# A transformer decoder on one core: copies and tables on ScalarE, reordered TensorE work, and probabilities transposed in two halves of 64 rows

## The chip, the cores and the metric

The kernel runs on one core of a Trainium2 chip. The metric is the device time of one execution in microseconds (us), the median of several runs. Engines are named as in the profile: PE (TensorE; PEld is its weight loading), DVE (VectorE), ACT (ScalarE), POOL (GpSimd), SP (SyncE, which issues the DMAs).

## The reference, cut to what matters

Two batches (B = 2) of 512 tokens with 128 channels pass through six blocks, each added to its input. Two of them have the windowed attention that the change is about: the first (here A) once, and the last (here F) in six layers, each layer followed by a gated feed-forward part on shifted tokens.

```python
def shift_tokens(t):
    a, s = jnp.split(t, 2, -1)
    s = jnp.pad(s, ((0, 0), (1, 0), (0, 0)))[:, :-1]
    return jnp.concatenate([a, s], -1)
...
for i in range(DEPTH):      # DEPTH = 6, HEADS = 16, DIM_HEAD = 64, WINDOW = 32
    x = attn_layer(shift_tokens(x), Wqkv[i], q_scale[i], k_scale[i], Wo[i]) + x
    x = ffn_layer(shift_tokens(x), ln_g[i], ln_b[i], W1[i], b1[i], W2[i], b2[i]) + x
```

`attn_layer` projects to q, k and v, normalises q and k per head, scales them (`q_scale`, `k_scale`), rotates them (with tables of cosine and sine times a position-dependent scale), and lets each token see itself and the 32 before it: scores, softmax, times v, then the output projection. `ffn_layer` is a layer norm, two projections to 341 columns (gate and up), gelu(gate) times up, and a projection back. All is fp32.

## The kernel before, in words

Tokens lie along the free axis: x is [128 channels, 2 x 512]. Block A is two units `("A", b)`, block F twelve units `(("F", l), b)`, one for each layer and batch. Each unit handles 16 heads as 8 pairs p (two heads of 64 channels are 128 partitions). Every engine runs its own program in a fixed order; semaphores join them (`wait_ge` on a mark that another engine's instruction sets). There is no planner: the order in each engine's function is the schedule. `take(pe, bank)` makes PE wait until the readers of a PSUM bank gave it back (`read`).

A unit has three parts. Line numbers are those of the kernel before.

**Projections** (`a_head_*`, `a_proj_*`). For each p PE makes q and k (`a_qk_pe`, L285 and L290, banks p % 2 and 2 + p % 2), now and then a block of v (`a_v_pe`, L274), and in F sums of squares (`a_ss_pe`, L331, bank 5). DVE multiplies q and k with the tables (`a_rope_dve`, L607, L608), SP swaps rows by DMA, POOL adds (L705, L706). Between them runs the feed-forward part of the unit before (`f_before`), placed by hooks: centre (L2015), variance (L2030), three gate/up pairs (`f_up_pe`, L2038 and L2040, banks 6 and 7), on ACT the gelu with table loads around it (L2105, L2109), on DVE `f_mul_dve` (L2159), which frees bank 7, and on PE `f_down_pe` (L2046, three accumulating matmuls to bank 7). Then ACT computes the inverse norms (L513, L515, L516, L518), and PE spreads them to all partitions for pair 0 (`a_spread_q_pe`, `a_spread_k_pe`, L339, rows of 32).

**Steps** (`a_steps_*`), for p = 0 to 7. PE adds the mask to an empty bank (`a_mask_pe`, L372 in 64x64 tiles, L367 for p = 7), adds the scores (`a_scores_pe`, L384, 64x64 tiles), spreads the norms of later pairs (L341, 32 rows, bf16), multiplies the probabilities of p-2 with v (`a_values_pe`, L415, tiles of 128 rows and 64 columns), transposes the probabilities of p-1 (`a_turn_pe`, L398, eight 128x128 transposes), and adds p-3 to the output projection (`a_out_pe`, L425). The mask waits for DVE's subtraction of p-1, the scores for q times its norm. DVE takes the row maximum (`a_top_dve`, L656), subtracts it (L659), multiplies the next pair's q with its norm (L621), sums the exponentials (L642) and inverts (L649). ACT copies k's norm (L534), makes the exponential (L542), copies the values (L547) and the two transposed banks (L554). POOL scales the probabilities (L714) and k (L698). Hooks of the steps: DVE adds the feed-forward result to x after p = 1 (`f_add_dve`, L2164), copies x shifted by one token into `xsh` after p = 3 (`move`, L2133 and L2134), and, for b = 1 and all but the last layer, builds the next layer's four rotation tables after p = 5 (`f_tab_dve`, L2171, four instructions).

**Tail** (`a_tail_*`). Values of p = 6, output of 5, q and k of the next unit's pair 0, transposes of p = 7 and so on, until DVE adds the unit's output to x (L689).

## Time and profile before

| | us |
|---|---|
| median of 3 runs (1751.57 to 1753.41) | 1751.95 |
| the profiled execution | 1752.89 |
| its span in the profile | 1751.1 |
| PE busy | 1573.1 (90%), x15445 |
| DVE busy | 1183.6 (68%), x2048 |
| ACT busy | 904.8 (52%), x1584 |
| POOL busy | 593.2 (34%), x552 |

Block F fills the span from about 830 us to the end, block A the first 150 us. A unit of F repeats almost exactly: measured from one first row maximum (L656, p = 0) to the next unit's, units with b = 0 take 76.3 us and those with b = 1 78.8 us. A matmul's duration in the profile includes its way through the array, so how long PE needs for a piece of work is read from starts: from the start of one group to the start of the next. A plain fp32 matmul appears as two passes ("x2"), a transpose as one.

### The profile page before, as it was taken

Reading aid. Unit: us, or ns where it says so; the run is one execution under the profiler, and the core shown is the slowest. Engines: PE = TensorE matmul, PEld = TensorE weight load, DVE = VectorE, ACT = ScalarE, POOL = GpSimd, SP = SyncE. Lnnn points to the kernel's source line nnn. Section 1 sums busy time; section 2 is a strip of 40 time slices with the busy share of each in tenths; the row PEclk is TensorE's granted clock in tenths of the full one; section 3 lists DMA queues with packets and bytes.
Section 4 is the critical chain, followed back from the end, with each engine's and each line's share of the span. In section 5 each row is a group of like instructions: output and inputs, shape, how many; then the busy total and the mean of one; then the engine's idle time right before and its main releaser. Section 6 shows DMA issues by size and latency. Waiting matters only on the chain.

```text
span 1751.1 us, 37919 instructions
## 1 busy us (share of the span) xinstructions
PE 1573.1 (90%) x15445; PEld 855.6 (49%) x15445; DVE 1183.6 (68%) x2048; ACT 904.8 (52%) x1584; POOL 593.2 (34%) x552
## 2 busy tenths in 40 slices
PE   7887569999999998779999999999999999999996
PEld 2645336565566554223645445363545545353543
DVE  5686576656566654347778778677877867787773
ACT  2435334344533443335665656666566666666663
POOL 5362000000000000105564655445465655555561
PEclk9899779999999999879999999999999999999998
DMA  7134100000000000203041322314142231314120
GB/s 248 28 118 193 54 0 7 2 21 1 21 21 1 21 1 1 93 1 122 30 145 60 96 99 70 129 33 135 56 125 82 86 125 31 127 65 131 68 64 13
DMA packets 50668, 119.41 MB, mean 68 GB/s; under 512 B 15297, under 2 KB 20161, under 8 KB 48321
## 3 DMA queue, kind: packets, MB, share of 16 engines
q1 hardware_dynamic: 50496, 116.99, 20.3%
q8 instruction: 125, 2.05, 0.5%
q14 instruction: 47, 0.38, 0.1%
HBM read 37.52 MB, written 0.52 MB: 22 GB/s over the span
## 4 chain that ended last, share of the span: by engine, by line
PE 52%; DVE 28%; ACT 9%; issue 5%; DMA 3%; POOL 2%; SPq 1%; DVEq 0%; ACTq 0%
DVE nm L656 4%; PE ps L1583 3%; DVE nm L642 3%; PE ps L285 3%; PE ps L425 3%; PE ps L415 3%; PE ps L290 3%; PE ps L1636 3%; PE ps L274 3%; DVE big L659 2%; PE ps L1645 2%; DMA big<-big 2%; DVE big L607 2%; PE ps L1602 2%; DVE big L608 2%
## 5 line engine op out<-in xcount | busy, mean ns | idle before, releaser
L714 POOL TENSOR_TENSOR big<-big,nm 128x384 f32<-128x384 f32 x224 | 189.7, 867 | 186.5 <-DVE nm L649 186.5
L705 POOL TENSOR_TENSOR big<-big 128x512 f32<-128x512 f32 x112 | 143.3, 1280 | 310.8 <-DMA big<-big 309.8
L607 DVE TENSOR_TENSOR big<-ps,big 128x512 f32<-128x512 f32 x224 | 153.7, 686 | 87.3 <-ACT sq L487 55.8
L542 ACT ACTIVATE big<-big 128x384 f32<-128x384 f32 x224 | 109.4, 522 | 126.7 <-DVE big L659 126.6
L1427 POOL MEMSET big<- 128x512 f32 x1 | 0.5, 526 | 489.0 <-DVE x L1910 489.0
L608 DVE TENSOR_TENSOR big<-ps,big 128x512 f32<-128x512 f32 x224 | 152.5, 681 | 0.0
L415 PE MATMUL ps<-big 128*64 128x64 f32 x3584 | 130.6, 226 | 23.1 <-ACT big L554 22.9
L415 PEld LDWEIGHTS ps<-big 128*64 128x64 f32 x3584 | 116.5, 139 | 63.5 <-ACT big L554 46.6
L706 POOL TENSOR_TENSOR big<-big 128x512 f32<-128x512 f32 x112 | 144.5, 1290 | 0.0
L1870 DVE TENSOR_TENSOR big<-ps,fix 128x512 f32<-128x512 f32 x192 | 119.2, 683 | 37.3 <-PE ps L1583 36.9
L398 PE MATMUL ps<-ident,big 128*128 128x128 f32 x896 | 129.3, 283 | 15.2 <-POOL big L714 13.2
L698 POOL TENSOR_TENSOR big<-big 128x512 f32<-128x512 f32 x84 | 107.2, 1276 | 71.7 <-ACT big L534 71.6
L656 DVE TENSOR_REDUCE nm<-ps 128x4 f32<-128x384 f32 x224 | 112.3, 543 | 26.9 <-PE ps L384 24.3
L554 ACT ACTIVATE big<-ps 128x512 f32<-128x512 f32 x224 | 122.3, 594 | 9.8 <-PE ps L398 8.0
L479 ACT ACTIVATE big<-ps 128x512 f32<-128x512 f32 x112 | 66.7, 595 | 112.8 <-PE ps L274 112.8
L398 PEld LDWEIGHTS ps<-ident,big 128*128 128x128 f32 x896 | 97.8, 142 | 40.5 <-POOL big L714 27.3
L659 DVE TENSOR_TENSOR big<-ps,nm 128x384 f32<-128x384 f32 x224 | 113.5, 549 | 0.3
L642 DVE TENSOR_REDUCE nm<-big 128x8 f32<-128x768 f32 x96 | 91.5, 953 | 21.8 <-ACT big L542 20.0
L274 PE MATMUL ps<-big,xsh 128*128 128x512 f32 x192 | 104.7, 628 | 0.0
L384 PE MATMUL ps<-big 64*64 64x96 f32 (+1 forms) x3584 | 97.3, 244 | 5.5 <-DVE big L627 2.2
L285 PE MATMUL ps<-xsh,big 128*128 128x512 f32 x192 | 100.6, 606 | 0.2 <-DVE big L608 0.2
L425 PE MATMUL ps<-fix,big 128*128 128x512 f32 x192 | 99.6, 600 | 0.7 <-ACT fix L547 0.7
(301 smaller groups left out, 2930.9 us busy)
## 6 DMA issues: line engine op xcount, KB each, us to landing
big<-big SPq DMA_DIRECT2D x224, 256.0 KB, 2.4
big<-big SPq DMA_DIRECT2D x112, 128.0 KB, 2.4
big<-in_F_w SPq DMA_DIRECT2D x6, 1536.0 KB, 7.0
big<-in_zero SPq DMA_DIRECT2D x8, 1088.0 KB, 12.5
big<-big SPq DMA_DIRECT2D x84, 64.0 KB, 2.0
big<-in_D_w SPq DMA_DIRECT2D x12, 256.0 KB, 3.0
big<-in_F_wo SPq DMA_DIRECT2D x6, 512.0 KB, 4.3
big<-in_F_w SPq DMA_DIRECT2D x6, 341.0 KB, 3.0
```

The source lines that it names most:

```text
L274: pe.matmul(ps[:, kv, :], src_of(key, b)[:, 128 * t:128 * t + 128], Wqkv[:, 2, 512 * hf:512 * hf + 512], start=True, stop=True).then_inc(* ...
L285: pe.matmul(ps[:, kq, :], Wqkv[:, 0, 128 * p:128 * p + 128], src_of(key, b), start=True, stop=True).then_inc(*full[kq].mark((key, b, "q", p)))
L398: last = pe.transpose(ps[:, 4 + h, 128 * j:128 * j + 128], P[:, 2 * (p % 2) + h, at0:at0 + 128], ident[:, :])
L415: last = pe.matmul(ps[64 * h:64 * h + 64, 6, 64 * m:64 * m + 64], vv[:, m // 2, 128 * p + 64 * h:128 * p + 64 * h + 64], PT[:, 2 * (p % 2) ...
L425: last = pe.matmul(ps[:, Y, :], Wo[:, p, :], ot(key, p), start=p == 0, stop=p == NP - 1)
L607: dve.tensor_tensor(tmp[:, i, w, :], ps[:, k, :], tb[:, 2 * w, :], ALU.mult).then_inc(*part.mark((key, b, p, 0)))
L608: dve.tensor_tensor(sinp[:, i, T * w:T * w + T], ps[:, k, :], tb[:, 2 * w + 1, :], ALU.mult).then_inc(*part.mark((key, b, p, 1)))
L642: dve.tensor_reduce(nm[:, i, 8:16].rearrange("p (h j) -> p h j", h=2), P[:, g:g + 2, :].rearrange("p h (j k) -> p h j k", j=4)[:, :, :, 0: ...
L656: dve.tensor_reduce(nm[:, i, 4 * h:4 * h + 4], s4(h), AX, ALU.max).then_inc(*topped.mark((key, b, p, h)))
L659: dve.tensor_tensor(shft[:, 2 * (p % 2) + h, :].rearrange("p (j k) -> p j k", j=4), s4(h), nm[:, i, 4 * h:4 * h + 4].unsqueeze(2).to_broad ...
L706: pool.tensor_tensor(KT[:, p, :], tmp[:, i, 1, :], swp[:, i, T:2 * T], ALU.add).then_inc(*k_added.mark((key, b, p)))
L714: pool.tensor_tensor(v, v, nm[:, p % 3, 16 + 4 * h:20 + 4 * h].unsqueeze(2).to_broadcast([128, 4, KW]), ALU.mult)\
```

## The change

What it does, part by part:

- **Transposes.** Each 128x128 transpose becomes two of 64 rows, one per half of the partitions (`tile_position` (0, 0) and (64, 0)), with the 64x64 part of the identity as moving operand. The upper half of all eight goes to bank 4, the lower half to bank 5, and both banks are marked full at the end. `a_values_pe` reads the new layout. This holds for A and F.
- **Fillers.** In F, `f_down_pe` is split: the first two matmuls after the spreads of pair 0, the third in the steps of p = 0, behind the scores and the spreads of pair 1. Both remaining v blocks (4 and 5) go ahead of the spreads. The next unit's first q is made before the values of p = 6, its k right after them, and the output of 6 goes behind q and k of pair 1.
- **Spreads.** From p = 1 on, the spreads of later pairs stand between mask and scores instead of behind the scores.
- **Banks.** The third up projection goes to bank 2 instead of 7.
- **ACT in place of DVE.** The two copies of `move` and the tables of the next layer are made by ACT (`f_move_act` after p = 3, `f_tab_act` after p = 4 and p = 5); the tables of layer 0 stay with DVE.
- **The feed-forward add.** `f_add_dve` moves from after p = 1 to before p = 0 on DVE.

Not shown: `a_qk_pe` is cut into `a_q_pe` and `a_k_pe`, which it now calls; the bank of an up projection is read from `UP` by `f_mul_dve` too; DVE's own table function marks `tab_first`; and the last unit's `f_down_pe` gets all three parts.

```diff
...
@@ -311,14 +317,13 @@
                 if "up" in hooks:
                     hooks["up"]()
                 a_ss_pe(pe, key, b, NP // 2 - 1)
-                a_v_pe(pe, key, b, 4)
+            a_v_pe(pe, key, b, 4)
+            a_v_pe(pe, key, b, 5)
+            if l2:
+                a_spread_q_pe(pe, key, b, 0)
+                a_spread_k_pe(pe, key, b, 0)
                 if "down" in hooks:
                     hooks["down"]()
-                a_spread_q_pe(pe, key, b, 0)
-                a_spread_k_pe(pe, key, b, 0)
-            else:
-                a_v_pe(pe, key, b, 4)
-            a_v_pe(pe, key, b, 5)
 
         def a_ss_pe(pe, key, b, g):
 
@@ -389,14 +394,19 @@
         def a_turn_pe(pe, key, b, p):
             for h in range(2):
                 pe.wait_ge(*scaled.at((key, b, p, h)))
-                if p == 0:
-                    take(pe, 4 + h)
-                else:
-                    pe.wait_ge(*turned.at((key, b, p - 1, h)))
                 for j in range(4):
                     at0 = 160 * j - (WIN if j % 2 else 0)
-                    last = pe.transpose(ps[:, 4 + h, 128 * j:128 * j + 128], P[:, 2 * (p % 2) + h, at0:at0 + 128], ident[:, :])
-                last.then_inc(*full[4 + h].mark((key, b, "t", p)))
+                    for c_ in range(2):
+                        if h == 0 and j == 0:
+                            if p == 0:
+                                take(pe, 4 + c_)
+                            else:
+                                pe.wait_ge(*turned.at((key, b, p - 1, c_)))
+                        rows = slice(64 * c_, 64 * c_ + 64)
+                        last = pe.transpose(ps[:, 4 + c_, 256 * h + 64 * j:256 * h + 64 * j + 64], P[rows, 2 * (p % 2) + h, at0:at0 + 128],
+                                            ident[rows, rows], tile_position=(64 * c_, 0))
+                        if (h, j) == (1, 3):
+                            last.then_inc(*full[4 + c_].mark((key, b, "t", p)))
 
         def a_values_pe(pe, key, b, p):
             for h in range(2):
@@ -413,7 +423,7 @@
                     vv = V if j % 2 else V2
                     for h in range(2):
                         last = pe.matmul(ps[64 * h:64 * h + 64, 6, 64 * m:64 * m + 64], vv[:, m // 2, 128 * p + 64 * h:128 * p + 64 * h + 64],
-                                         PT[:, 2 * (p % 2) + h, 128 * j + 64 * c_:128 * j + 64 * c_ + 64], start=True, stop=True,
+                                         PT[:, 2 * (p % 2) + c_, 256 * h + 64 * j:256 * h + 64 * j + 64], start=True, stop=True,
                                          tile_position=(0, 64 * h))
             last.then_inc(*full[6].mark((key, b, "o", p)))
 
@@ -429,17 +439,20 @@
         def a_steps_pe(pe, key, b, l2, late):
             for p in range(NP):
                 a_mask_pe(pe, key, b, p, l2)
+                if l2 and p >= 2 and p + 2 < NP:
+                    a_spread_k_pe(pe, key, b, p + 2)
+                if l2 and 0 < p < NP - 1:
+                    a_spread_q_pe(pe, key, b, p + 1)
                 a_scores_pe(pe, key, b, p, l2)
-                if l2 and p + 1 < NP:
-                    a_spread_q_pe(pe, key, b, p + 1)
                 if l2 and p == 0:
+                    a_spread_q_pe(pe, key, b, 1)
                     a_spread_k_pe(pe, key, b, 1)
+                if p in late:
+                    late[p]()
                 if p < 2:
                     a_v_pe(pe, key, b, NT + 2 + p)
-                if l2 and p + 2 < NP:
-                    a_spread_k_pe(pe, key, b, p + 2)
-                if p in late:
-                    late[p]()
+                    if l2:
+                        a_spread_k_pe(pe, key, b, p + 2)
                 if p >= 2:
                     a_values_pe(pe, key, b, p - 2)
                 if p >= 1:
@@ -448,16 +461,18 @@
                     a_out_pe(pe, key, b, p - 3)
 
         def a_tail_pe(pe, key, b, l2, nxt):
+            if nxt:
+                a_q_pe(pe, *nxt, 0)
             a_values_pe(pe, key, b, NP - 2)
+            if nxt:
+                a_k_pe(pe, *nxt, 0)
             a_out_pe(pe, key, b, NP - 3)
-            if nxt:
-                a_qk_pe(pe, *nxt, 0)
             a_turn_pe(pe, key, b, NP - 1)
-            a_out_pe(pe, key, b, NP - 2)
             if nxt:
                 a_qk_pe(pe, *nxt, 1)
                 if v_with(l2, 1) is not None:
                     a_v_pe(pe, *nxt, v_with(l2, 1))
+            a_out_pe(pe, key, b, NP - 2)
             a_values_pe(pe, key, b, NP - 1)
             if nxt:
                 a_qk_pe(pe, *nxt, 2)
@@ -597,6 +612,8 @@
         def a_rope_dve(dve, key, b, p, l2):
             tb = tab if l2 else tab0
             i, n = slot(b, p), NP * b + p - 3
+            if l2 and n == -3 and key[1] > 0:
+                dve.wait_ge(*tab_made.at((key[1], 1)))
             if n >= 0:
                 dve.wait_ge(*k_added.at((key, n // NP, n % NP)))
             for w, (k, part, squared_) in enumerate(((p % 2, q_part, q_sq), (2 + p % 2, k_part, k_sq))):
@@ -675,6 +692,8 @@
                     a_rest_dve(dve, key, b)
                     a_q_norm_dve(dve, key, b, 0)
                     a_parts_dve(dve, key, b)
+                if "down" in early:
+                    early["down"]()
                 for p in range(NP):
                     a_top_dve(dve, key, b, p)
                     if l2 and p + 1 < NP:
...
@@ -2028,6 +2047,8 @@
             pe.wait_ge(*squared.at(("F1", l, b)))
             take(pe, 7)
             pe.matmul(ps[:, 7, :], mean_m[:, :], fsq, start=True, stop=True).then_inc(*full[7].mark(("F1", l, b, "var")))
+
+        UP = (7, 7, 2)
 
         def f_up_pe(pe, l, b, i):
             c0, m = DIC[i]
@@ -2036,15 +2057,18 @@
                 pe.wait_ge(*affine.at(("F", l, b)))
             take(pe, 6)
             pe.matmul(ps[0:m, 6, :], W1[:, DI + c0:DI + c0 + m], fxn, start=True, stop=True).then_inc(*full[6].mark(("F", l, b, "gate", i)))
-            take(pe, 7)
-            pe.matmul(ps[0:m, 7, :], W1[:, c0:c0 + m], fxn, start=True, stop=True).then_inc(*full[7].mark(("F", l, b, "up", i)))
-
-        def f_down_pe(pe, l, b):
-            take(pe, Y)
-            for i, (c0, m) in enumerate(DIC):
+            take(pe, UP[i])
+            pe.matmul(ps[0:m, UP[i], :], W1[:, c0:c0 + m], fxn, start=True, stop=True).then_inc(*full[UP[i]].mark(("F", l, b, "up", i)))
+
+        def f_down_pe(pe, l, b, parts):
+            for i in parts:
+                if i == 0:
+                    take(pe, Y)
+                m = DIC[i][1]
                 pe.wait_ge(*f_mul.at((l, b, i)))
                 last = pe.matmul(ps[:, Y, :], W2[0:m, i, :], fh[0:m, i, :], start=i == 0, stop=i == 2)
-            last.then_inc(*full[Y].mark(("F", l, b, "f2")))
+            if i == 2:
+                last.then_inc(*full[Y].mark(("F", l, b, "f2")))
 
         def f_before(l, b):
 
@@ -2055,7 +2079,7 @@
             if u is None:
                 return {3: lambda: f0_centre_pe(pe), 4: lambda: f0_var_pe(pe)}, {}
             return ({3: lambda: f_centre_pe(pe, *u), 4: lambda: f_var_pe(pe, *u), 6: lambda: f_up_pe(pe, *u, 0), 7: lambda: f_up_pe(pe, *u, 1),
-                     "up": lambda: f_up_pe(pe, *u, 2), "down": lambda: f_down_pe(pe, *u)}, {})
+                     "up": lambda: f_up_pe(pe, *u, 2), "down": lambda: f_down_pe(pe, *u, (0, 1))}, {0: lambda: f_down_pe(pe, *u, (2,))})
 
         F_UNITS = [(("F", l), b) for l in range(LAYERS) for b in range(B)]
 
...
@@ -2108,16 +2132,32 @@
         def f_exp_table(act):
             act.preload_act_table_set("natural_log_exp_and_others")
 
+        def f_move_act(act, l, b):
+            act.wait_ge(*x_new.at(("Ff", l, b)))
+            step(act, act_step, act.activation(xsh[0:64, b, :], x[0:64, cols(b)], ACT.Copy))
+            act.activation(xsh[64:128, b, 1:T], x[64:128, T * b:T * b + T - 1], ACT.Copy).then_inc(moved, 1)
+
+        def f_tab_act(act, l, i):
+            act.wait_ge(scl_in, 16 * (l + 1))
+            act.wait_ge(*k_part.at((("F", l - 1), B - 1, NP - 1, 1)))
+            for j in (2 * i, 2 * i + 1):
+                ins = act.activation(tab[:, j, :], tab0[:, j, :], ACT.Copy, scale=scl[:, i:i + 1])
+            ins.then_inc(*tab_made.mark((l, i)))
+
         def f_act_hooks(act, key, b):
             u = f_before(key[1], b)
             if u is None:
                 return {3: lambda: f0_square_act(act), 4: lambda: f0_root_act(act)}, {}
 
+            l, late = key[1], {3: lambda: f_move_act(act, *u)}
+            if b == B - 1 and l + 1 < LAYERS:
+                late[4], late[5] = lambda: f_tab_act(act, l + 1, 0), lambda: f_tab_act(act, l + 1, 1)
+
             def last():
                 f_gelu_act(act, *u, 2)
                 f_exp_table(act)
             return ({3: lambda: f_square_act(act, *u), 4: lambda: f_root_act(act, *u), 5: lambda: f_xn_act(act, *u), 6: lambda: f_gelu_act(act, *u, 0),
-                     7: lambda: f_gelu_act(act, *u, 1), "up": last}, {})
+                     7: lambda: f_gelu_act(act, *u, 1), "up": last}, late)
 
         def f_act(act):
             act.wait_ge(*zeroed.at("F"))
...
@@ -2180,17 +2220,11 @@
             def multiply():
                 f_mul_dve(dve, *u, 1)
                 f_mul_dve(dve, *u, 2)
-
-            def move():
-                dve.wait_ge(*x_new.at(("Ff", *u)))
-                shift_dve(dve, u[1], (moved, 1))
             if u is not None:
-                early = {4: lambda: f_scale_dve(dve, *u), 6: lambda: f_mul_dve(dve, *u, 0), 7: multiply}
-                late[1], late[3] = lambda: f_add_dve(dve, *u), move
+                early = {4: lambda: f_scale_dve(dve, *u), 6: lambda: f_mul_dve(dve, *u, 0), 7: multiply,
+                         "down": lambda: f_add_dve(dve, *u)}
             else:
                 early[5] = lambda: f0_scale_dve(dve)
-            if b == B - 1 and l + 1 < LAYERS:
-                late[5] = lambda: f_tab_dve(dve, l + 1)
             late[NP + 2] = lambda: f_shift_dve(dve, l, b)
             return early, late
 
@@ -2245,7 +2279,7 @@
                     f_ff_sp(sp, l)
                 attn_sp(sp, ("F", l), 1, True)
                 if l + 1 < LAYERS:
-                    sp.wait_ge(*tab_made.at(l))
+                    sp.wait_ge(*(tab_made.at((l, 1)) if l else tab_first.at(0)))
                     f_w_sp(sp, l + 1)
         A_UNITS = [("A", b) for b in range(B)]
         block = c.enter_context(nc.Block())
```

## Rows read from the trace of the kernel before

**Rows 1.** The page, busy tenths in 40 slices: the granted clock of PE.
```profile
PEclk9899779999999999879999999999999999999998
```
**Rows 2.** PE's waits from 840 us on, longest first: engine, line, releaser: us, times, longest.
```profile
PE ps L415 <- ACT big L554: 19.7, 41, 1.1
```
**Rows 3.** Timeline of PE, one step of a unit with b = 0: start us, us, what.
```profile
1311.49 0.36 PE L372 MATMUL ps<-band,identb 64*64 64x384 bf16 x4
1311.68 0.83 PE L384 MATMUL ps<-big 64*64 64x64 f32 x32
1312.44 0.39 PE L341 MATMUL ps<-xn,big 32*128 32x512 bf16 x2
1312.76 1.15 PE L415 MATMUL ps<-big 128*64 128x64 f32 x32
1313.85 1.09 PE L398 MATMUL ps<-ident,big 128*128 128x128 f32 x8
1314.77 1.02 PE L425 MATMUL ps<-fix,big 128*128 128x512 f32 x2
1315.73 0.36 PE L372 MATMUL ps<-band,identb 64*64 64x384 bf16 x4
```
**Rows 4.** Durations by source line, ns min/median/max, of weight loads and matmuls.
```profile
L398 PEld LDWEIGHTS ps<-ident,big x896: 137/140/230, 47.8 to 1719.4; 128*128 128x128 f32 x180
L398 PE MATMUL ps<-ident,big x896: 272/273/476, 47.8 to 1719.5; 128*128 128x128 f32 x180
L415 PEld LDWEIGHTS ps<-big x3584: 132/138/227, 51.5 to 1721.6; 128*64 128x64 f32 x200
L415 PE MATMUL ps<-big x3584: 222/222/366, 51.5 to 1721.7; 128*64 128x64 f32 x200
L1560 PEld LDWEIGHTS ps<-big x144: 186/192/192, 274.5 to 661.1; 128*128 128x128 f32 x144
```
**Rows 5.** Timelines in block D: loads of 128x128 under 64-column matmuls; matmuls in 64-row halves.
```profile
342.25 1.31 PEld L1560 LDWEIGHTS ps<-big 128*128 128x128 f32 x11 [0.24 <-issue]
...
270.01 0.39 PE L1543 MATMUL ps<-big 64*128 64x128 f32 x4
270.23 0.39 PE L1547 MATMUL ps<-big 64*128 64x128 f32 x4
```
**Rows 6.** Timeline of DVE: tables of a b = 1 unit, then steps of a b = 0 unit.
```profile
1241.68 2.78 DVE L2171 TENSOR_SCALAR big<-big 128x512 f32<-128x512 f32 x4
...
1295.36 1.02 DVE L656 TENSOR_REDUCE nm<-ps 128x4 f32<-128x384 f32 x2 [0.41 <-PE ps L384]
...
1303.62 0.70 DVE L2164 SCALAR_TENSOR_TENSOR x<-ps,big,x 128x512 f32<-128x512 f32 x1
...
1312.11 0.94 DVE L2134 COPY xsh<-x 64x511 f32<-64x511 f32 x1
...
1325.71 1.02 DVE L656 TENSOR_REDUCE nm<-ps 128x4 f32<-128x384 f32 x2 [0.54 <-PE ps L384]
...
1341.05 0.69 DVE L689 TENSOR_TENSOR x<-x,ps 128x512 f32<-128x512 f32 x1 [1.52 <-PE ps L425]
```
**Rows 7.** Timelines of PE and ACT, end of the projections (same unit).
```profile
1286.12 1.09 PE L2040 MATMUL ps<-xc,big 128*85 128x512 f32 x2 [0.98 <-DVEq L136]
1289.10 2.74 PE L2046 MATMUL ps<-fix,big 128*128 128x512 f32 x6
1291.77 1.13 PE L339 MATMUL ps<-rs,big 32*128 32x512 f32 x4
...
1285.97 1.28 ACT L2109 ACT_TABLE_LOAD   x1
1288.28 0.69 ACT L513 ACTIVATE rs<-ps,eps 128x512 f32<-128x512 f32 x1 [1.03 <-PE ps L331]
```
**Rows 8.** Timeline of PE, start of the tail (same unit).
```profile
1327.62 1.02 PE L425 MATMUL ps<-fix,big 128*128 128x512 f32 x2
1329.78 1.15 PE L415 MATMUL ps<-big 128*64 128x64 f32 x32 [1.14 <-ACT big L554]
```

More of the change, by code:

```diff
@@ L281, in a_qk_pe, with a_k_pe @@
             if p < 2:
-                take(pe, kq)
+                take(pe, p)
             else:
                 pe.wait_ge(*q_part.at((key, b, p - 2, 1)))
-            pe.matmul(ps[:, kq, :], Wqkv[:, 0, 128 * p:128 * p + 128], src_of(key, b), start=True, stop=True).then_inc(*full[kq].mark((key, b, "q", p)))
+            pe.matmul(ps[:, p % 2, :], Wqkv[:, 0, 128 * p:128 * p + 128], src_of(key, b), start=True, stop=True).then_inc(*full[p % 2].mark((key, b, "q", p)))
+        def a_k_pe(pe, key, b, p):
+            kk = 2 + p % 2
             if p < 2:
@@ L2070, in f_pe @@
                 f_up_pe(pe, *u, i)
-            f_down_pe(pe, *u)
+            f_down_pe(pe, *u, range(3))
         def f_square_act(act, l, b):
@@ L2156, in f_mul_dve @@
             m = DIC[i][1]
[L2157 removed]
+            dve.wait_ge(*full[UP[i]].at(("F", l, b, "up", i)))
             dve.wait_ge(*gg.at((l, b, i)))
[L2159 to L2160 removed]
+            dve.scalar_tensor_tensor(fh[0:m, i, :], ps[0:m, UP[i], :], b1[0:m, i:i + 1], fg[i % 2][0:m, :], ALU.add, ALU.mult).then_inc(*f_mul.mark((l, b, i)))
+            read(dve, UP[i], f_mul, (l, b, i))
         def f_add_dve(dve, l, b):
```

15 lines of the change are left out of this document (7 added, 8 removed).

## The prediction

> **What bounds the kernel now.** I read the granted clock first: it is at or near full in block F, so PE runs at its 2.4 GHz level there and nothing below rests on the clock [rows 1]. Then the timeline of PE inside a step [rows 3], PE's waits [rows 2], the timeline of DVE over a unit [rows 6], and the two seams, end of projections [rows 7] and start of the tail [rows 8].
>
> The step from 1311.49 to 1315.73 has no gap: PE alone needs 4.24 us (mask 0.19, scores 0.76, spreads 0.32, values 1.09, transposes 0.92, output 0.96) [rows 3]. DVE needs about 3.6 us for its five operations. So from p = 3 on PE is the bound, except where DVE has extras: the add, 0.70 [rows 6], the two copies, about 1.4 with 0.94 for the second [rows 6], the tables, 2.78 [rows 6]. Before p = 3 the chain mask, scores, maximum, subtraction, exponential bounds. In projections and tail PE is nearly always at work, apart from 0.98 us ahead of the third up projection (units with b = 0) [rows 7] and 1.14 us ahead of the tail's first values [rows 8]; PE's waits for ACT's transposed copies sum to only 19.7 us over block F [rows 2]. An edit therefore pays if it shortens PE's work or fills a gap of it; DVE relief pays only where DVE's extras top 4.24.
>
> **Transposes.** Now eight pass in 0.92 us [rows 3], about 0.109 each. What sets 0.109? A matmul with 128 moving columns lasts 272, one with 64 lasts 222 ns [rows 4]: 50 ns for 64 columns, 107 for 128. A load lasts 140 here, 138 for 64 columns of v, but 192 for 128 columns in a plain fp32 matmul [rows 4]. So, less a common start of about 85, a transpose's load takes only some 53 ns, and streaming, 107, is the bound. Halves stream 64 columns, and two halves run side by side: in block D pairs of 64-row matmuls with 128 columns each leave every 0.11 us (four in 0.22) [rows 5]. Per pair both load and stream are then 53 ns. The nearest row is the values: 16 pairs of 64-column loads and streams in 1.09 us with one or two changes of tiling, near 0.058 per pair [rows 3]. Eight pairs: 0.46 instead of 0.875, minus 0.41. Ends: eight loads at the plain price, eleven starting in 1.31 us with the last one's 0.19, so 0.112 each, under matmuls of 64 columns that could leave faster [rows 5], make 0.90 (no gain); and the same with no overlap of the halves, 16 x 0.112 = 1.79. Below 0.43 nothing speaks for it. I take 0.46, since the load in question is the one with the 140 ns row.
>
> The Trainium skill speaks against this edit: "TensorE: Matmul & The Clock Gate", section "LDWEIGHTS (loading the stationary operand)", gives a load as columns / 1.2 whatever its rows, 107 ns for each half. The 140 against 192 ns disagrees with it for transposes; by the rule the turn would stay near 0.88 and the kernel would come out as in the first rival.
>
> **Changes of tiling.** The pieces of a step without them are 0.16 + 0.66 + 0.21 + 0.93 + 0.875 + 0.857 = 3.69 (the 0.857 and the 0.16 from streaming 1024 + 1024 and 384 columns at 2.4 GHz), so four changes cost 0.55, 0.14 each [rows 3]. A step gains two: transposes to output, and the spreads now stand inside the 64x64 work. Plus 0.28. A full step on PE becomes 4.24 + 0.28 - 0.41, about 4.10.
>
> **Steps of a unit with b = 0.** Intervals between the maxima of successive p, before 4.66, 4.44, 3.65, 4.96, 3.77, 4.44, 4.43 (sum 30.35, 1295.36 to 1325.71 [rows 6]). After:
> - p0 to 1: 3.90. The add is gone; subtraction done at 1.90, q norm 2.57, then the spread that now precedes the scores 0.35, scores 0.92.
> - 1 to 2: 4.13. Here ACT has v, norm and exponential in a row.
> - 2 to 3: 3.89 as the first. These two chains lose 0.25 each to the spread in front.
> - 3 to 4: 4.40, PE's 4.10 and 0.3 in which the values wait for ACT's copies, which start only when both banks are full.
> - 4 to 5 and 5 to 6: 4.10 and 4.13. The copies cost nothing on DVE; on ACT they, and then the tables (two of some 0.6 in each of two steps), fit into its idle time behind exponential, values and transposed copies: 3.1 of 4.1 us. If that cover were gone it would cost 0.2 a step; I charge 0.1 in b = 1 units. Their waits are long met: the add to x stands before p = 0, the scales were loaded some 10 us earlier, and the rotation that now waits for ACT's tables comes 15 us after them. SP's wait ahead of the next weights is for tables made a layer before, so nothing queues behind it.
> - 6 to 7: 4.43 - 0.21 (no spread) - 0.41 = 3.80.
> Sum 28.35: minus 2.00. With b = 1 the interval 5 to 6 was longer by the tables (6.41, next 3.80; sum 31.68): minus 3.3.
>
> **Ahead of the steps.** The bank change removes the 0.98 wait (b = 0) [rows 7]. The table load ends at 1287.25; Relu, Ln and Exp take 2.3, the inverse norms are there at 89.6 instead of 90.6. PE has finished v 4 and 5 by 88.9 and waits 0.7 for them: the down matmuls (2.67 [rows 7]) that covered this now lie behind. Spreads 1.06, two down matmuls 1.71, mask 0.3: scores at 92.7 instead of 94.4. Then the new wait: DVE's add precedes the first maximum and waits for the third down matmul, which follows scores (0.81) and spreads (0.35); with 1.15 to its end and 0.8 for the add the maximum starts at 95.9 instead of 95.36: plus 0.5. Behind that wait sit maximum, subtraction, exponential, and through them mask 1. In a b = 1 unit there was no 0.98 to win, so plus 1.6. Ends: 0 if the add slips in early, +2.2 if nothing ahead is won.
>
> **Tail.** The next q (0.857) fills the gap, which the ACT chain keeps: minus 0.86 [rows 8]. Transposes of 7: minus 0.41, two changes plus 0.28 and 0.02. Maximum 7 to the add of the unit, 15.34 [rows 6], becomes 14.37: minus 0.97.
>
> **Sum.** b = 0, layers 1 to 5: 5 x (0.51 - 2.00 - 0.97) = -12.3. b = 1, layers 0 to 4: 5 x (1.63 - 3.3 - 0.9) = -12.9. First unit (no feed-forward before it) -1.2, last (no tables, no successor) -0.5, block A's two units -1: together -28. From the profiled 1752.89 (1.8 above its span of 1751.1, 0.9 above the median) 1724.9; from the median 1724. I say **1725**.
>
> **Rivals.**
> 1. *The loads bound the halves.* A half's load costs what L1560's does, 0.112 a pair, or the halves pass one after the other at 0.057 each: transposes stay at 0.90. Each step bounded by PE is then 4.24 + 0.28 + 0.02 = 4.54, the unit saves 0.4 and the last loses: 1750 (1744 to 1757). For it: the load is still 128 columns wide, and no row shows a transpose at 64 rows. Against it: 140 ns. Chance 0.15.
> 2. *Serial halves with plain loads* (slower). 1.79 per transposing group, 1.33 above my 0.46, in four steps and the tail, five times in twelve units: plus 80, 1805. This decides from 0.93 us per group on; there all gains are eaten. Against it: the four half-row matmuls in 0.22 us [rows 5]. Chance 0.09, in which I also count a longer wait of the first maximum behind the add.
> 3. My forecast: 0.76, own range 1710 to 1740 (0.04 per change of tiling is 5 us over the block; 0.05 per turn 3; the first maximum 6).
>
> A measurement of this kernel can tell about 0.2%, 3.5 us, from no change. Faster takes nearly all of the forecast and 0.04 of rival 1: 0.80; the same 0.06; slower 0.14 (0.05 of rival 1, rival 2). The range reaches from 1708 into rival 1, to 1752, which leaves under 2 in 10 out.
>
> **What would show it.** Right: L398's matmuls doubled to 1792, near 222 ns each, loads at 140; a group start to output of 0.6; steps at 4.1; no idle time of PE ahead of the third up projection and of the tail's values; L2164 just before the first maximum, with PE's third down as releaser; the first maximum 0.5 or 1.6 later against the unit's start. Wrong: loads at 190, or group starts 0.9 apart or more; ACT as releaser of values in every step, which would say that the tables or the late full marks have made it the bound.

## The result and the profile after

| | before | after |
|---|---|---|
| median, both measured together (7 runs each) | 1751.57 us | 1767.94 us |
| range of the runs | 1750.13 to 1755.76 | 1759.21 to 1771.42 |
| the profiled execution, its span | 1752.89, 1751.1 | 1768.36, 1766.5 |

The ratio is 1.0077, 95% interval 1.0056 to 1.0098: the change makes the kernel 0.8% slower. Forecast were 1725 us and "faster".

The clock row of the page of the changed kernel, then the same row of experiment e2, to which the text comes back:

```profile
PEclk9999579999999998778989899999999899989998
```
```profile
PEclk9999579999999999779999999999999999999998
```

Before, the right half, block F, was all nines [rows 1]. Now it has eights inside it in four places, and in e2 in none. The view by stretches shows how little an average tells (columns: us, busy time of PE, PEld, DVE, ACT, POOL with counts, granted clock as a share of 2.4 GHz, DMA share, GB/s). Block F of before, then of after:

```profile
840.00:1700.00 860.00, 809.18 (x8300) 425.65 (x8301) 651.71 (x1144) 536.98 (x947) 468.27 (x436) 1.00 0.27 89
```
```profile
840.00:1700.00 860.00, 819.32 (x8820) 413.94 (x8816) 628.39 (x1077) 549.30 (x970) 459.07 (x426) 0.96 0.27 89
```

PE's waits of after from 840 us on (us in total, times, longest), to be read against [rows 2]:

```profile
PE ps L377 <- DVE big L676: 20.4, 11, 1.9
PE ps L425 <- ACT big L569: 7.0, 24, 0.8
PE ps L2061 <- DVEq L136: 6.8, 5, 2.4
```

The values (L425) wait far less than before: 7.0 us instead of 19.7. At the head of the list stands a wait of the mask (L377) for DVE's subtraction (L676), 1.9 us once in each of eleven units. The timelines of DVE and PE there, in a unit with b = 0 of after (start us, us, what, idle time before and its releaser):

```profile
1308.21 0.75 DVE L2204 SCALAR_TENSOR_TENSOR x<-ps,big,x 128x512 f32<-128x512 f32 x1 [1.98 <-PE ps L2069]
1309.11 1.02 DVE L673 TENSOR_REDUCE nm<-ps 128x4 f32<-128x384 f32 x2
1310.05 1.01 DVE L676 TENSOR_TENSOR big<-ps,nm 128x384 f32<-128x384 f32 x2
```
```profile
1308.97 0.39 PE L346 MATMUL ps<-xn,big 32*128 32x512 bf16 x1
1311.21 0.36 PE L377 MATMUL ps<-band,identb 64*64 64x384 bf16 x4 [1.85 <-DVE big L676]
1311.71 0.40 PE L346 MATMUL ps<-xn,big 32*128 32x512 bf16 x1
1312.04 1.56 PE L389 MATMUL ps<-big 64*64 64x64 f32 x32
1313.53 2.02 PE L274 MATMUL ps<-big,xsh 128*128 128x512 f32 x2
```

DVE's add (L2204) waited 1.98 us for the third down matmul (L2069), so maximum and subtraction come late, and PE, which has nothing left but mask 1, stands still for 1.85 us. Then the same 32 score matmuls take 1.56 us that take 0.83 in [rows 3], and two passes of v 2.02 instead of some 1.1. The stretches say why:

```profile
1306.00:1309.40 3.40, 3.35 (x43) 1.48 (x35) 1.28 (x3) 0.92 (x2) 1.27 (x1) 1.00 0.27 59
1309.40:1312.80 3.40, 1.45 (x27) 1.00 (x31) 3.37 (x7) 1.86 (x4) 1.28 (x1) 0.88 0.26 58
1312.80:1316.20 3.40, 3.27 (x24) 1.23 (x18) 2.58 (x6) 0.60 (x1) 1.61 (x2) 0.62 0.02 5
```

In the second stretch, which has the gap in it, PE was busy 1.45 us of 3.40; some 0.8 us after the gap, at about 1312.0, its granted clock fell to the 1.2 GHz level. 0.88 and 0.62 are means over stretches that hold both levels. In this unit it stayed there 3.4 us, in others 10.2 us, once in the steps of ten of the eleven units that have the gap. Before has no such stretch in the steps of any unit, but for the first 2 us of the first, where one from the block ahead ends. The eleventh, the fourth unit of F, is a control within the same execution. It has the gap, and the clock stays at full:

```profile
1073.82 0.36 PE L377 MATMUL ps<-band,identb 64*64 64x384 bf16 x4 [1.85 <-DVE big L676]
```
```profile
1072.00:1075.40 3.40, 1.43 (x37) 0.94 (x37) 3.37 (x7) 1.87 (x4) 1.27 (x1) 1.00 0.27 58
```

Its seven intervals from maximum to maximum sum to 29.03 us. The ten others take 29.8 to 31.9.

### The profile page after: what moved, and what is told of

Its sections match the earlier page's. It is cut to its first block, busy times and chain, and to the rows that moved or that the text cites. A ratio compares the mean times of both kernels' runs of the same rounds, so it can differ in the third digit from the quotient of the medians.

```text
span 1766.5 us, 39604 instructions
## 1 busy us (share of the span) xinstructions
PE 1599.0 (91%) x16341; PEld 849.4 (48%) x16341; DVE 1172.8 (66%) x2006; ACT 926.3 (52%) x1626; POOL 593.0 (34%) x552
## 4 chain that ended last, share of the span: by engine, by line
PE 63%; DVE 18%; ACT 11%; issue 4%; DMA 2%; POOL 2%; SPq 1%; DVEq 0%; ACTq 0%
PE ps L425 5%; PE ps L435 5%; PE ps L389 4%; PE ps L1602 3%; PE ps L284 3%; PE ps L406 3%; PE ps L292 3%; PE ps L274 3%; PE ps L1655 3%; PE ps L1664 2%; DVE nm L673 2%; PE ps L1621 2%; DVE big L624 2%; DMA big<-big 2%; DVE big L625 2%
## 5 line engine op out<-in xcount | busy, mean ns | idle before, releaser
L733 POOL TENSOR_TENSOR big<-big,nm 128x384 f32<-128x384 f32 x224 | 185.3, 849 | 174.1 <-DVE nm L666 174.1
L425 PE MATMUL ps<-big 128*64 128x64 f32 x3584 | 135.0, 231 | 12.0 <-ACT big L569 11.3
L425 PEld LDWEIGHTS ps<-big 128*64 128x64 f32 x3584 | 120.7, 143 | 46.5 <-ACT big L569 30.2
L676 DVE TENSOR_TENSOR big<-ps,nm 128x384 f32<-128x384 f32 x224 | 113.2, 547 | 0.0
L274 PE MATMUL ps<-big,xsh 128*128 128x512 f32 x192 | 113.0, 675 | 0.0
L389 PE MATMUL ps<-big 64*64 64x96 f32 (+1 forms) x3584 | 108.0, 260 | 1.4 <-DVE big L644 1.4
L435 PE MATMUL ps<-fix,big 128*128 128x512 f32 x192 | 104.6, 627 | 0.7 <-ACT fix L562 0.7
L406 PE MATMUL ps<-ident,big 64*128 64x64 f32 x1792 | 93.5, 241 | 9.5 <-POOL big L733 8.4
L389 PEld LDWEIGHTS ps<-big 64*64 64x64 f32 x3584 | 88.5, 144 | 24.9 <-issue 22.7
```

Of the source, the lines that this page charges most:

```text
L274: pe.matmul(ps[:, kv, :], src_of(key, b)[:, 128 * t:128 * t + 128], Wqkv[:, 2, 512 * hf:512 * hf + 512], start=True, stop=True).then_inc(* ...
L389: last = pe.matmul(ps[64 * c_:64 * c_ + 64, h, KW * j + k0:KW * j + KW], Q[rows, p, 64 * m:64 * m + 64], KT[rows, p, 64 * m - WIN + k0:64 ...
L406: last = pe.transpose(ps[:, 4 + c_, 256 * h + 64 * j:256 * h + 64 * j + 64], P[rows, 2 * (p % 2) + h, at0:at0 + 128], ident[rows, rows], t ...
L425: last = pe.matmul(ps[64 * h:64 * h + 64, 6, 64 * m:64 * m + 64], vv[:, m // 2, 128 * p + 64 * h:128 * p + 64 * h + 64], PT[:, 2 * (p % 2) ...
L435: last = pe.matmul(ps[:, Y, :], Wo[:, p, :], ot(key, p), start=p == 0, stop=p == NP - 1)
L733: pool.tensor_tensor(v, v, nm[:, p % 3, 16 + 4 * h:20 + 4 * h].unsqueeze(2).to_broadcast([128, 4, KW]), ALU.mult)\
```

## Where the time went, by parts of block F

Each kernel's DVE timeline gives the first maximum of each unit, the maxima of p = 1 to 7 and the unit's last add. From them: the time from F's first maximum to its last add; the seven intervals of the steps, mean over units 2 to 12; the head, from a unit's last add to the next unit's first maximum, mean by the b of the unit it leads into; and the granted clock from 840 to 1700 us. The tail was 15.3 us before. With the new tail it is 14.44 (14.58 in e8), and 14.47 in e4 and e6, which have whole transposes. Each row is one execution, and not always a typical one: those of e10 and e5 took 6.8 and 4.9 us less than the median of their kernel, those of e7, e8 and e12 6.9, 5.2 and 3.8 us more.

| kernel | F | steps | head, b = 1 | head, b = 0 | clock |
|---|---|---|---|---|---|
| before | 894.2 | 30.97 | 30.73 | 31.90 | 1.00 |
| after | 910.8 | 30.87 | 32.72 | 34.34 | 0.96 |
| e1 | 882.1 | 30.91 | 30.26 | 31.92 | 0.98 |
| e2 | 877.6 | 29.02 | 32.37 | 32.52 | 1.00 |
| e3 | 897.6 | 30.83 | 31.08 | 32.70 | 1.00 |
| e4 | 921.1 | 30.82 | 33.83 | 35.13 | 0.98 |
| e5 | 875.0 | 30.38 | 30.33 | 31.54 | 1.00 |
| e6 | 893.8 | 30.86 | 31.39 | 32.83 | 1.00 |
| e7 | 879.5 | 29.53 | 31.26 | 32.77 | 0.99 |
| e8 | 906.9 | 30.33 | 32.38 | 35.17 | 0.99 |
| e9 | 930.2 | 32.00 | 32.48 | 36.22 | 0.95 |
| e10 | 881.0 | 28.53 | 32.38 | 34.38 | 1.00 |
| e11 | 868.9 | 28.88 | 31.05 | 32.92 | 1.00 |
| e12 | 884.2 | 29.55 | 32.38 | 32.65 | 1.00 |

After is 16.6 us longer in F than before. F starts 1.3 us later, and what follows its last add is 2.5 us shorter; together that is the 15.4 us between the two spans.

## Experiments

The kernels were measured in three sessions (e1 to e4, e5 to e8, e9 to e12), before again in each: 1753.46, 1754.45 and 1754.98 us. The ratios are to these.

Theory 1: the add ahead of the first maximum opens the gap ahead of mask 1, and the lower clock behind the gap costs more than all else gains. If so, anything that closes the gap must bring the kernel below before. Theory 2: the new order itself loses the time, and the clock only goes with it. Theory 3: the halves let the clock fall.

**e1: the add back behind p = 1.**

```diff
-                early = {..., "down": lambda: f_add_dve(dve, *u)}
+                early = {...}
+                late[1] = lambda: f_add_dve(dve, *u)
```

> The changed kernel with one edit: DVE's feed-forward add goes back from before p = 0 to after p = 1. Theory 1 (the add in front of the first maximum leaves PE without work for about 2 us at the end of p = 0, and the granted clock falls behind that): the gap of PE ahead of the mask of p = 1 goes, the granted clock stays at full over block F (mean about 0.96 as before the change), the steps of p = 0 to 2 take 4.1, 4.9 and 3.9 us instead of 4.5, 5.2 and 3.8 or more, and the time falls to 1730 (1722 to 1740). Theory 2 (the spreads in front of the scores and the moved down matmuls lose the time themselves, the clock only goes with it): the time stays at 1750 or more though the clock is full. Theory 3 (half-height transposes keep the array less busy and let the clock fall): the clock stays at 0.93 to 0.94 and the time above 1760.

Measured: 1738.28, ratio to before 0.9915 (0.990 to 0.993). The time is as expected, the way there is not. The gap ahead of mask 1 is gone, but ACT now waits 1.29 us for v, whose matmul stands behind the third down matmul. Exponential and sum come late, the first interval is 5.51 us and not 4.1, and PE has a gap of 1.24 us ahead of the first transposes. Behind it the clock was at half for 3.4 us in eight of twelve units:

```profile
1297.01 0.46 PE L406 MATMUL ps<-ident,big 64*128 64x64 f32 x8 [1.24 <-POOL big L733]
```
```profile
1297.40:1300.80 3.40, 3.08 (x50) 1.96 (x46) 2.83 (x5) 2.59 (x5) 2.65 (x4) 0.57 0.14 28
```

**e2: the gap filled, order untouched.** Two dummy matmuls whose product nobody reads, at the end of p = 0.

```diff
+                if l2 and p == 0:
+                    pe.wait_ge(*v_ready.at((key, b, 4)))
+                    for _ in range(2):
+                        pe.matmul(ps[:, 4, :], mean_m[:, :], tab0[:, 0, :], start=True, stop=True)
```

> The changed kernel with the order kept, and two matmuls of 128x512 on constants, whose result nobody reads, added at the end of p = 0 in every unit of block F, where PE waits for DVE (1.7 us of work in a gap of 1.9). Nothing is taken from the computation. Theory 1: the granted clock stays full, and the time falls by what the half clock costs, some 2 us in each of twelve units: 1742 (1735 to 1750); what remains above the kernel with the add behind p = 1 is the wait itself. Theory 2: clock full, but the time stays at 1760 or more. Theory 3: the clock still falls in every unit.

Measured: 1735.82, ratio 0.9894 (0.988 to 0.9908). The same place of the step in e2's PE timeline, and its stretches:

```profile
1286.61 1.98 PE L459 MATMUL ps<-big,mean_m 128*128 128x512 f32 x4
1288.53 0.36 PE L377 MATMUL ps<-band,identb 64*64 64x384 bf16 x4
...
1289.35 0.89 PE L389 MATMUL ps<-big 64*64 64x64 f32 x32
```
```profile
1286.00:1289.40 3.40, 3.25 (x15) 1.03 (x14) 3.25 (x7) 2.18 (x4) 1.72 (x2) 1.00 0.27 58
1289.40:1292.80 3.40, 3.19 (x56) 1.85 (x55) 3.26 (x7) 1.29 (x3) 1.63 (x3) 1.00 0.02 5
```

More work on PE and 32 us less time. The order of all other work is that of after, and DVE's add still waits (1.97 us here for 1.98); what differs is that PE has work in the gap, and its clock. That is against theory 2.

**e9: the filler elsewhere.** Is it the place, or just another matmul in the program? One dummy matmul of the same shape behind the values of p = 4, none in the gap.

```diff
+                if l2 and p == 4:
+                    pe.matmul(ps[:, 4, :], mean_m[:, :], tab0[:, 0, :], start=True, stop=True)
```

> The changed kernel with one dummy 128x512 fp32 matmul (0.86 us of PE, used by nobody) in p = 4, behind the values, where PE is the bound, and none in the gap ahead of mask 1. Theory 1 (the gap of some 2 us ahead of mask 1 and the half clock behind it are the loss): it stays; 1768 plus 12 x 0.86 = 1778, between 1768 and 1788, with stretches at half clock in nearly every unit. Rival (the dummy matmuls of the earlier run helped in another way than by standing in the gap, as by moving the code or by more work for PE in a unit): 1736 to 1750.

Measured: 1784.53, ratio 1.0166 (1.0149 to 1.0184). In one unit of it:

```profile
1474.42 0.53 PE L377 MATMUL ps<-band,identb 64*64 64x384 bf16 x4 [1.85 <-DVE big L678]
...
1483.29 1.63 PE L425 MATMUL ps<-big 128*64 128x64 f32 x32
```
```profile
1474.00:1477.40 3.40, 2.98 (x38) 1.97 (x39) 2.37 (x5) 0.84 (x2) 2.22 (x3) 0.52 0.28 63
1477.40:1480.80 3.40, 3.40 (x19) 1.25 (x19) 2.20 (x5) 1.56 (x4) 0.64 (x2) 0.50 0.00 0
1480.80:1484.20 3.40, 3.40 (x56) 2.41 (x56) 1.96 (x4) 1.93 (x5) 2.62 (x4) 0.50 0.79 203
```

The gap of 1.85 us is back, and so is the clock of 0.50, here for 10 us; in eight of the eleven units with the gap it falls in the steps. The rival is out.

**e7: the gap closed a third way.** All three down matmuls ahead of the first mask, so that the add has nothing to wait for behind the scores.

```diff
-   "down": lambda: f_down_pe(pe, *u, (0, 1))}, {0: lambda: f_down_pe(pe, *u, (2,))})
+   "down": lambda: f_down_pe(pe, *u, range(3))}, {})
```

> The changed kernel with all three down matmuls ahead of the first mask; DVE's add stays in front of the first maximum. Theory 1 (it is the wait for the third down matmul behind the scores that opens the gap, not the add as such): the scores of p = 0 start 0.9 us later, the first maximum 1.3 us earlier, the gap ahead of the mask of p = 1 shrinks to under 0.6 us, the clock stays full, and the time is 1733 (1726 to 1742). If the add's place alone were the cause: the clock still falls, 1760 or more.

Measured: 1733.14, ratio 0.9884 (0.9864 to 0.9904). Three different edits (e1, e2, e7) gain 30, 32 and 35 us over after, each a gain over before. Theory 1 stands for the gap and the clock; how much of the loss is the clock's comes below.

**e3, e4, e6: what the halves are worth.** e3 is before with the halves alone (`a_turn_pe` and `a_values_pe` of after), e4 is after without them, e6 is e5 (below) without them.

> The kernel before with the transposes in halves of 64 rows and nothing else. All theories: a group of sixteen takes 0.71 us to the next group instead of 0.92. Theory 1 and 2: the clock stays as before (0.96), the time falls by 0.2 us in each step that PE bounds and in the tail, some 0.8 a unit: 1742 (1737 to 1748). Theory 3: the clock falls in the steps, and the time is 1752 or more.

> The changed kernel with transposes of 128 rows as before. Theory 1: the clock falls in each unit as in the changed kernel (0.93), and the steps and the tail get 0.2 us longer each: 1780 (1773 to 1788). Theory 2: the same within 5 us. Theory 3: the clock comes back to 0.96 and the time to 1755 or less.

> The kernel of the run before this one with transposes of 128 rows. What the halves are worth in this order: the steps that PE bounds take 4.39 instead of 4.21 us, some 0.6 us a unit, 7 us in all: 1731 (1726 to 1738). A rival says that they are worth nothing as when put alone into the kernel before, because other work bounds: within 3 us of the run before.

Measured: e3 1758.38, ratio 1.0028 (1.0019 to 1.0036); e4 1781.57, 1.016 (1.0135 to 1.0185); e6 1750.82, 0.998 (0.9968 to 0.9992). So the halves cost 3 to 6 us in the old order (1742 was expected), and gain 14 and 15 us in the new one. Theory 3 is out: in e3 the clock in F is full but for one stretch of 3.4 us, and in e4, without halves, it falls behind the gap in eight of eleven units.

The steps are as they should be. In the old order only the last two intervals of a b = 0 unit are bounded by PE enough to shrink (4.44 and 4.43 become 4.33 and 4.24); in the new order four intervals do (4.72, 4.39, 4.39, 4.11 in e6; 4.62, 4.21, 4.24, 3.93 in e5), 0.61 a unit, about 7 us in all, as e6's expectation has it. The means in the table differ by 0.49 only, because e5's last unit has 3.4 us at half clock. (Between after and e4 they don't differ, 30.87 and 30.82: after spends more of its steps at half clock.)

The rest, two thirds of the 18.9 us between e6 and e5 in F, lies in the heads, where no transpose is. (The medians differ by 15.2 us; e5's profiled execution was its fastest.) The timelines of DVE and POOL of e3 at the start of a head show one thing that happens there:

```profile
1188.87 0.69 DVE L694 TENSOR_TENSOR x<-x,ps 128x512 f32<-128x512 f32 x1 [1.52 <-PE ps L430]
1189.70 1.25 DVE L2138 COPY xsh<-x 64x512 f32<-64x512 f32 x1
1190.99 1.38 DVE L2139 COPY xsh<-x 64x511 f32<-64x511 f32 x1
```
```profile
1188.18 1.27 POOL L710 TENSOR_TENSOR big<-big 128x512 f32<-128x512 f32 x1 [9.19 <-DMA big<-big]
1189.41 1.27 POOL L711 TENSOR_TENSOR big<-big 128x512 f32<-128x512 f32 x1
1190.63 1.45 POOL L710 TENSOR_TENSOR big<-big 128x512 f32<-128x512 f32 x1
```

DVE's two shifted copies at the end of a unit, 0.42 us each when alone, meet POOL's sums for the next unit and take 1.25 and 1.38. By source line over block F (count, ns min/median/max), the second copy of before (all uses of the line), after, e2, e6; then the first copy of e5 and e6:

```profile
L2134 DVE COPY xsh<-x x23: 424/426/940, 876.3 to 1725.1; 64x511 f32<-64x511 f32 x23
```
```profile
L2174 DVE COPY xsh<-x x11: 1377/1379/1414, 879.7 to 1669.5; 64x511 f32<-64x511 f32 x11
```
```profile
L2178 DVE COPY xsh<-x x12: 424/902/1382, 875.8 to 1707.5; 64x511 f32<-64x511 f32 x12
```
```profile
L2171 DVE COPY xsh<-x x12: 424/1388/1395, 878.9 to 1725.7; 64x511 f32<-64x511 f32 x12
```
```profile
L2175 DVE COPY xsh<-x x12: 418/419/1424, 874.3 to 1703.9; 64x512 f32<-64x512 f32 x12
L2170 DVE COPY xsh<-x x12: 418/1432/1475, 877.4 to 1725.3; 64x512 f32<-64x512 f32 x12
```

Behind them queue the rotations of the next unit, and the centre matmul of the feed-forward part waits for the copy. The second copy is slow in e5 as in e6 (median 1380 and 1388 ns). It is the first that tells the two apart: 0.42 us in eight of the eleven heads of e5, 1.37 or more in ten of e6's. With b = 1 its delay passes into the head one for one: 30.10 us in the heads of e5 with a first copy of 0.42, 31.11 in the one with 1.42. Whether POOL's sums and the copies meet depends on shifts of under a microsecond.

The copies don't explain all. In e3 they meet POOL in three of the six heads with b = 1, and these are 0.2 to 1.7 us longer than the other three. The five with b = 0 have copies of 0.42 and still lose 0.80 us on average; in two of them POOL waits 5.8 and 5.5 us for a transfer, where no such wait was over 3.1 in before. What delays that transfer is open. The rival of e6, "within 3 us", is refuted; my 7 us were right for the steps and left the heads out.

**e5: add late, and the third down matmul behind v 6 and the spreads of pair 2.**

```diff
+                late[1] = lambda: f_add_dve(dve, *u)        # instead of "down"
...
-                if p in late:
+                if p in late and not (l2 and p == 0):
                     late[p]()
                 if p < 2:
                     a_v_pe(pe, key, b, NT + 2 + p)
                     if l2:
                         a_spread_k_pe(pe, key, b, p + 2)
+                if p in late and l2 and p == 0:
+                    late[p]()
```

> The changed kernel with two edits: DVE's add after p = 1, as in the first experiment, and PE's third down matmul at the very end of p = 0, behind v block 6 and the spread of pair 2. If the order in p = 0 is what costs (theory 1): the interval from the first to the second maximum falls from 5.51 to 4.66 us, since ACT's copies of v and k's norm come earlier again; a unit takes 74.5 (b = 1) to 75.5 us (b = 0), no gap of PE over 1 us is left in it, the clock stays full, and the time is 1724 (1718 to 1732). If the heads' transfers bound the units instead, the gain comes back there and the time stays at 1735 or more.

Measured: 1735.61, ratio 0.9899 (0.988 to 0.9918); 1724 missed. Its heads are, with e1's, the shortest, 2.0 us under e2's with b = 1, but only 1.0 with b = 0, and the steps give 1.4 back. The first maximum is no longer late, so the exponential of p = 0 now queues on ACT behind the copies of v and of k's norm; DVE waits 1.00 us for it, as it does in e7, and the first interval is 4.65 instead of 3.84.

**e8, e12: ACT's part.** e8 is e2 with copies and tables back on DVE; e12 is e2 with only the copies back.

> The kernel with the two matmuls that fill the gap, and with the shifted copies and all tables back on DVE (after p = 3 and p = 5). What ACT's taking over is worth once the clock is full: interval 3 to 4 becomes 4.97 instead of 4.62 with the next one shorter, and in b = 1 units the interval 5 to 6 grows by 2 us: 2.2 us in b = 1 units, 0.2 in the others: 1748 (1743 to 1754). A rival (PE bounds these steps anyway): 1736 to 1740.

> The changed kernel with the filler in the gap and only the shifted copies back on DVE; the tables stay on ACT. Of the 28 us that both cost together the intervals of the last profile give the copies 0.15 us a unit and the tables 2.2 us in each unit with b = 1 that makes tables: so 1735.8 plus 2 to 4: 1739, between 1736 and 1744. Rival (it is the copies, the second of which takes 1.38 us beside GpSimd's additions, that push the head behind them back): 1750 or more.

Measured: e8 1764.19, ratio 1.0059 (1.0043 to 1.0075); e12 1742.53, 0.9931 (0.9913 to 0.9949). In F the copies cost 6.6 us (12 times 0.53 in the steps) and the tables 22.7: five times 1.85 us in one interval, and five times 2.5 us in the head that follows, into the next layer (35.17 against 32.65). Together 29 us where I had priced 12 (e8's rival is out too); e12 lies within the 1736 to 1744 expected of it, and its rival is out. The head's 2.5 us isn't the tables' own time: in each of these five heads of e8 the second copy meets POOL (1.38 us, in e12 0.42), and in two PE's clock is at half for 3.4 us. Both profiled executions also show some 6 us more than e2 ahead of F. The medians don't: e12's is 6.7 us and e8's 28.4 us above e2's, which F alone accounts for.

**e10, e11: the place of the spreads.** e10 is e2, and e11 is e7, with the spreads of the steps behind the scores again.

```diff
                 a_mask_pe(pe, key, b, p, l2)
+                a_scores_pe(pe, key, b, p, l2)
                 if l2 and p >= 2 and p + 2 < NP:
                     a_spread_k_pe(pe, key, b, p + 2)
                 if l2 and 0 < p < NP - 1:
                     a_spread_q_pe(pe, key, b, p + 1)
-                a_scores_pe(pe, key, b, p, l2)
```

> The changed kernel with the filler in the gap, and the spreads of the steps behind the scores again instead of between mask and scores. Theory 1 with its prices (0.14 us for a change of tiling, and 0.3 us of spreads ahead of the scores in the three first, chain-bound intervals): the full step on PE 4.21 becomes 4.07, four intervals of a unit, and the three first ones lose 0.25 each: 12 x (0.56 + 0.75) = 16 us less than 1735.8, so 1720, between 1716 and 1728. Rival (the place of the spreads is neutral, or it was good, since the q norm on DVE waits for them): 1733 to 1742.

> The changed kernel with all three down matmuls ahead of the first mask and the spreads behind the scores. Theory 1: the gain of e10 on top of 1733.1 (e7): 1718, between 1712 and 1726. Rival (what e7 wins in the steps the heads give back, waiting for their transfers): 1728 to 1736.

Measured: e10 1743.01, ratio 0.9937 (0.9922 to 0.9953), where 1720 was expected; e11 1724.78, 0.9839 (0.9819 to 0.9858), within its range. The PE timeline of e10 has the full step, 4.05 us from mask to mask instead of e2's 4.21:

```profile
1305.20 0.36 PE L377 MATMUL ps<-band,identb 64*64 64x384 bf16 x4
1305.39 0.83 PE L389 MATMUL ps<-big 64*64 64x64 f32 x32
1306.15 0.39 PE L346 MATMUL ps<-xn,big 32*128 32x512 bf16 x2
1306.47 1.15 PE L425 MATMUL ps<-big 128*64 128x64 f32 x32
1307.55 0.71 PE L406 MATMUL ps<-ident,big 64*128 64x64 f32 x16
1308.19 1.12 PE L435 MATMUL ps<-fix,big 128*128 128x512 f32 x2
1309.25 0.36 PE L377 MATMUL ps<-band,identb 64*64 64x384 bf16 x4
```

One change of tiling fewer, 0.16 us less. Yet the steps of a unit gain only 0.5 (the interval 1 to 2 grows by 0.2, the last by 0.3), and the heads into the next layer lose 1.9 (34.38 against 32.52): F of e10 is 3.4 us longer than F of e2, and that in e10's fastest execution; the medians differ by 7.2 us. Why, at one such head, first e2, then e10, the second copy and the sums of POOL:

```profile
1254.98 0.42 DVE L2178 COPY xsh<-x 64x511 f32<-64x511 f32 x1
...
1256.41 1.28 POOL L728 TENSOR_TENSOR big<-big 128x512 f32<-128x512 f32 x1 [2.69 <-DMA big<-big]
...
1260.87 1.27 POOL L728 TENSOR_TENSOR big<-big 128x512 f32<-128x512 f32 x1 [1.94 <-DMA big<-big]
```
```profile
1256.30 1.46 POOL L728 TENSOR_TENSOR big<-big 128x512 f32<-128x512 f32 x1 [0.88 <-DMA big<-big]
1256.67 1.38 DVE L2178 COPY xsh<-x 64x511 f32<-64x511 f32 x1
...
1265.79 1.27 POOL L728 TENSOR_TENSOR big<-big 128x512 f32<-128x512 f32 x1 [6.61 <-DMA big<-big]
```

In e10 the copy meets the sum; the rotations behind it start a microsecond late, and a later pair of sums waits 6.61 us for its transfer instead of 1.94. SP issues that pair's swap just around the loads of the next weights, so a late rotation is paid for several times over. That the weights are what holds the transfer up I did not test.

In e11 the same edit does pay, 8 us over e7. There the second copy met POOL in every head already (median 1383 ns in e7), so that loss could not be added. e11 is the fastest kernel here, 1.6% below before.

## Why the prediction was wrong, point by point

**The step that failed** is in the first paragraph: "it is at or near full in block F, so PE runs at its 2.4 GHz level there and nothing below rests on the clock". That was read off a profile in which PE never stood still for long at that place. I did see the wait that the change adds ("DVE's add precedes the first maximum and waits for the third down matmul", "Behind that wait sit maximum, subtraction, exponential, and through them mask 1") and priced it as lateness of the first maximum. I did not ask what PE does meanwhile. It does nothing for 1.85 us, and in ten of eleven units it then works at 1.2 GHz. After against e2, which differ by the filler alone: 33.2 us in F, of which the steps are 22 and the heads 11.2. In the steps 20.3 us stand in the units with the gap; the rest is in the first unit, where half clock from the block ahead lasts to 844 us (831 in e2). So the clock costs some 20 us directly. In the heads the clock is full but for 3.4 us in one; there after's second copy meets POOL in all eleven, e2's in the six with b = 1 only. That the shifted steps cause those meetings is likely, and not shown on its own. The same wait with PE busy costs what I said.

The 0.09 of rival 2 counted "a longer wait of the first maximum behind the add". The wait was not longer than priced, so "slower", to which I gave 0.14 in all, came by a way that no rival of mine had.

**Terms that held.** With the clock out of the way (e2 against before, in F):

| term, a unit | predicted | e2 |
|---|---|---|
| head, b = 1 | +1.6 | +1.64 |
| head, b = 0 | +0.5 | +0.62 |
| seven intervals | 28.35 (b = 0), 28.38 (b = 1) | 29.02 |
| tail with the unit's add | 14.37 | 14.44 |
| a full step on PE | 4.10 | 4.21 |
| transposes to output | 0.60 | 0.64 |

The sum for F was -26.9; e2 gives -16.6. The 10.3 us between them are nearly all in the intervals: 11 x 0.66 is 7.3, the first unit's another 1.6, the tails 0.8, the heads 0.6. Mis-sized are the intervals 1 to 2 (4.39 for 4.13, the chain through ACT) and 3 to 4 (4.61 for 4.40, values waiting for ACT's copies), and each full step by 0.1, since a change of tiling cost 0.16 and not 0.14, and the turn, with its change, 0.04 more. Of the tail's gain the halves give 0.03 (14.47 in e6), not 0.11.

**The halves.** Rivals 1 and 2 are both out. By source line of after:

```profile
L406 PEld LDWEIGHTS ps<-ident,big x1792: 134/139/226, 47.5 to 1737.0; 64*128 64x128 f32 x200
L406 PE MATMUL ps<-ident,big x1792: 221/223/366, 47.5 to 1737.0; 64*128 64x64 f32 x200
```

Twice the number of [rows 4], 139 and 223 ns, as foretold; sixteen pass in 0.64 us (1307.55 to 1308.19 above), less the change of tiling some 0.48. The rule of the Trainium skill that I set against the edit ("TensorE: Matmul & The Clock Gate", "LDWEIGHTS (loading the stationary operand)": columns / 1.2 for each load) would give no gain; the measurement decides against it, for transposes. What they are worth to the kernel is another matter: 0.6 us a unit in the steps, net of the added change (e5 and e6), and 1.1 to 1.3 in the heads, to which I had given nothing, by way of the first copy where b = 1.

**Copies and tables on ACT.** "The copies cost nothing on DVE" is wrong by 0.53 a unit, and of the tables I saw the 1.85 in their interval but not the 2.5 in the head behind it. These terms I had inside the sum of the intervals, so they changed what the parts are worth, not the total.

**The 0.98 wait** ahead of the third up projection was to vanish. In e2 it did. In after the stall moved to the second up projection (L2061, five times, up to 2.4 us, in the waits above): these are the heads with b = 0, where DVE, which frees bank 7, is late behind the slow copy. The kernel of e10, with the same slow copy there, has the stall too (1.4 to 2.3 us), and e12, with copies of 0.42 there, has none.

**Outside F** I gave block A -1. Unit ("A", 0) gained 3.8 us (from 68.2 to 64.3), and what follows up to F lost 5.4, at a clock of 0.90 from 500 to 840 us instead of 0.92. From kernel to kernel this part, the same code in all but for A's second unit, varies by up to 9 us (before has the least, e8 and e12 the most); why is open.

## What to carry to other kernels

Where an edit makes an engine wait, ask what TensorE does in that time: a gap of under 2 us was followed here by up to 10 us at half the clock, and it and what it shifted cost more than the whole change had gained. A filler matmul, or the order that needs none, cost nothing in such a place (e2, e7). And price the head that follows as well: an edit that shifts a phase by half a microsecond can make two engines meet, or a transfer queue behind another, in work that the edit never touches.

## What the runs showed of the hardware

- **The clock can fall after short gaps.** PE idle for 1.85 us ahead of mask 1, in a kernel that keeps PE over 90% busy: granted clock 0.50 for 3.4 or 10.2 us, in 10 of 11 units of after and 8 of 11 each of e4 and e9. In e1 a gap of 1.24 us ahead of the first transposes was followed by a stretch of 3.4 us as well, in eight of twelve units. A gap makes it likely, not certain: e10 has five of 1.35 to 2.30 us in its heads, before has one of 1.13 us in the tail of each unit with b = 0, and the clock stays full behind all of them.
- **DVE's copies beside POOL.** A copy of 64x511 from SBUF to SBUF takes 0.42 us alone and 1.38 beside a POOL addition, whose own time goes from 1.27 to 1.46; DVE's rotations, which read PSUM, keep their 0.68 beside the same additions. The Trainium skill ("SBUF — State Buffer", section "SBUF: two separate sides") has DVE and GpSimd share a pair of ports that one takes for a whole instruction while the other is blocked, if DVE's instruction is one that needs the pair; a copy of fp32 within SBUF is. The trace fits that: the copy that starts at 1256.67 ends at 1258.05, 0.29 us after the addition that held 1256.30 to 1257.76.
- **A change of tiling on PE** cost 0.16 us here, from 4.21 (e2) against 4.05 us (e10) for the same work with one change fewer.
